# Moving the load of a group's raw weight half from the middle of the following iteration's transfers to the end of an iteration

## The chip, the cores and the metric

The kernel runs on one core of a Trainium2 chip. The metric is device microseconds of one execution. Before the change the median of three runs is 1696.12 us (1695.85 to 1698.0).

## The reference

Two layers of gated cross attention with feed-forward blocks work on `x` (4 batches of 256 tokens, 256 wide) and a context of 1601 tokens per batch. The change lies in the first layer's attention. Cut to what matters:

```python
ln_out = _ln(hidden_states, ln_w, ln_b)
q  = _ln(_fp8_linear_pertensor(ln_out, wq, ...).reshape(b, s, g, hpg, d), qln_w, qln_b)    # 8 groups, 2 heads each, d = 128
k  = _ln(_fp8_linear_pertensor(ln_out, wk, ...).reshape(b, s, g, d), kln_w, kln_b)
v  = _fp8_linear_pertensor(ln_out, wv, ...).reshape(b, s, g, d)
core = _gqa(q, k, v)                                      # softmax(q k^T / sqrt(d)) v over the 256 own tokens
qx = _ln(_fp8_linear_pertensor(ln_out, wqx, ...), qxln_w, qxln_b)
kx, vx = jnp.split(jnp.einsum('bsi,oi->bso', cond, w_kv_x), 2, axis=-1)
xout = _gqa(qx, _ln(kx, kxln_w, kxln_b), vx)              # over the 1601 context tokens
cat = jnp.concatenate([core, xout], axis=-1)
return jnp.einsum('bsi,oi->bso', _div_clamp_fp8(cat, proj_smooth), wproj) * (proj_in_scale * proj_w_scale)
x = x + jnp.tanh(g_xattn[0]) * that
```

The second layer, the mixture of experts and the last feed-forward come after this attention and aren't touched.

## The kernel before

The attention is a software pipeline over `NGB` = 32 pairs of a group of heads and a batch. In the first 16 pairs batches 0 and 1 alternate, so that one group's weights serve two iterations. Each iteration makes the keys, queries and values of the following pair (`it + 1`), and works through the four softmax rounds n = 4·it to 4·it + 3 of its own pair, 128 query rows each against 1601 + 256 keys.

The probabilities of a round lie in `PB[n % 2]` as two bf16 parts. They have to be turned before TensorE can multiply them with the values: `turn_p(n, h)` is a transposing DMA issued from SyncE (L976) that writes half h of round n (h = 0: 16 blocks of 128 x 128, h = 1: 14 blocks) into `PT`. TensorE's `times_v(k, h)` (L1758, 24 matmuls for h = 0 and 21 for h = 1) takes rounds 2k and 2k + 1 together, and waits for `pt{h}_in0` and `pt{h}_in1`, which those DMAs raise. So `times_v(2 it + 1, 0)`, which TensorE meets in iteration it + 1 right after its second group of query projections (L1691), needs `turn_p(4 it + 3, 0)`, which SyncE issues at the start of its iteration it + 1.

Weights come from memory as float32 and have to be split into two bf16 parts once per group. For groups 2 to 7 that is done in halves of 512 columns: `sp_load_half` (L428) loads 512 KB into the single buffer `rawh`; ScalarE (L719, L721, L732, L743), VectorE (L626, L628) and, for the key half, GpSimd (L541, L543) write the two parts into a buffer that the trace calls `acc`; `sp_store_half` (L439 and L440 for the key half, L442 for the query half) stores them to `w_split`. From there `load_weights` (L931) fetches them into `wsb` when their group is due. There are 12 such half loads, one in each of the iterations 0 to 11. A half may be loaded only when the half before it has been split: `sp_load_half` waits on `w_hi`, `w_lo_dve`, `w_hi_pool` and `w_lo_pool`. VectorE's last split of an iteration stands ahead of its last `p_lo` of round 4 it + 2, on which `turn_p(4 it + 2, 1)` waits, and GpSimd's stands ahead of its `split_self` for the same round.

In SyncE's program an iteration is written out by hand. It issues, in this order: `turn_p(4 it - 1, 0)` and `(4 it - 1, 1)`; the V part of the weights if a new group follows; the store of the split half; the load of the next raw half; the K part; `turn_p(4 it, 1)`, `(4 it, 0)`, `(4 it + 1, 0)`; the rows of key norms out and back (L948, L961); the projection weights (L939, every second iteration); `turn_p(4 it + 1, 1)`, `(4 it + 2, 0)`, `(4 it + 2, 1)`; and in the iterations 8 to 19 a context store (L482). All of these go into the one DMA queue of SyncE.

Of the kernel before, what the change touches and what calls it, by code (L numbers as in the profile page):

```python
# [302 lines left out]
def flat(t):  # L303
    return t.rearrange("p a b -> p (a b)")
# [45 lines left out]
def wait_split(e, s, g, keys):  # L350

    e.wait_ge(s["w_hi"], parts_before(g + 1) if not keys else parts_before(g) + 6)
    e.wait_ge(s["w_hi_pool"], plain_before(g + 1))
    e.wait_ge(s["w_lo_dve"], parts_before(g + 1) if not keys else parts_before(g) + 6)
    e.wait_ge(s["w_lo_pool"], plain_before(g + 1))
# [66 lines left out]
def sp_load_half(e, m, s, g, keys):  # L422
    if keys and g > 2:
        wait_split(e, s, g - 1, False)
    elif not keys:
        wait_split(e, s, g, True)
    c0 = CK if keys else CQ
    e.dma_start(m.rawh, m.A["w_all"][g][:, :, c0:c0 + 512]).then_inc(s[f"w_in{int(not keys)}"], 16)  # L428


def sp_store_weights(e, m, s, g):
    wait_split(e, s, g, False)
    e.dma_start(m.w_split[g], (m.wsb if g == 0 else m.wo)[:, :]).then_inc(s["w_out"], 16)


def sp_store_half(e, m, s, g, keys):
    wait_split(e, s, g, keys)
    if keys:
        e.dma_start(m.w_split[g][:, 0:1024], m.woh[:, 0:1024]).then_inc(s["w_out"], 16)  # L439
        e.dma_start(m.w_split[g][:, 3072:4096], m.woh[:, 1024:2048]).then_inc(s["w_out"], 16)  # L440
    else:
        e.dma_start(m.w_split[g][:, 1024:3072], m.woh).then_inc(s["wq_out"], 16)  # L442
# [9 lines left out]
def sp_load_piece(e, m, s, b, i, part):  # L452

    ic, a, z = PIECES[i]
    if part == 0:
        if i == 0 or b == 3:
            e.wait_ge(s["pa_full"], made(first_of(2) - 4 + b, "V3"))
            e.wait_ge(s["ctx_out"], 64 * (b - 1))
        if i:
            wait_split(e, s, G - 1, False)  # L460
            e.wait_ge(s["wq_out"], 16 * (G - 2))
            e.wait_ge(s["ctx_lo_pool"], pieces_before(b, 0))
    k = (0, (z - a + 1) // 2, z - a)
    e.dma_start(ctx_piece(m, b, i)[0][:, k[part]:k[part + 1]], m.A["ctxT"][:, ic, b, a + k[part]:a + k[part + 1]]).then_inc(
        s[f"ctx_in{i}"], 16)
# [19 lines left out]
def sp_store_inputs(e, m, s, j):  # L485
    e.wait_ge(s["xq_done"], j + 1)
    at = QUANT[j % 4] * IC * S
    e.dma_start(m.inputs_d[j // 4][:, at:at + IC * S].rearrange("p (i s) -> p i s", i=IC),
                quantised(m, j)).then_inc(s[f"xq_out{j % 2}"], 16)
# [326 lines left out]
SPLITS = 2 * (G - 2)  # L816
# [19 lines left out]
def group_of(it):  # L836
    return it // 2 if it < PAIRS else it % G
# [7 lines left out]
def new_group(it):  # L845

    return it >= PAIRS or it % 2 == 0


def groups_taken(it):  # L850

    return it // 2 + 1 if it < PAIRS else it - PAIRS // 2 + 1


def made(it, what):

    at = ORDER.index(what)
    if it >= NGB:
        return len(ORDER) * NGB - LAG + it - NGB + 1
    missing = min(it, LAG) + (it < LAG and at >= ORDER.index("PR"))  # L860
    return len(ORDER) * it + at + 1 - missing
# [26 lines left out]
def raw_projection(m, i):  # L888

    return m.wpr[:, :] if i < NGB - 1 else m.rawh.rearrange("p i c -> p (i c)")  # L890
# [28 lines left out]
def sp_attention(e, m, s):  # L919
    w_at = (0, 2 * IC * 256, 2 * IC * 768, 2 * IC * WCOLS)  # L920

    def load_weights(it, which):
        if not 0 < it < NGB or not new_group(it):
            return
        e.wait_ge(s["pa_full"], made(it - 1, ("K3", "Q1", "V3")[which]))
        if it < PAIRS and which == 0:
            e.wait_ge(s["w_out"], 32 * group_of(it) if it > 2 else 32)
        elif 2 < it < PAIRS and which == 1:
            e.wait_ge(s["wq_out"], 16 * (group_of(it) - 1))
        a, b = w_at[which], w_at[which + 1]  # L930
        e.dma_start(m.wsb[:, a:b], m.w_split[group_of(it)][:, a:b]).then_inc(s[("ld_k", "ld_q", "ld_v")[which]], 16)  # L931

    def load_projection(i):
        if not 0 <= i < NGB or not new_group(i):
            return
        if 0 < i < NGB - 1:
            e.wait_ge(s["pw_lo"], groups_taken(i) - 1)
        c = 2 * HPG * group_of(i)
        e.dma_start(raw_projection(m, i), flat(m.A["wprojT"][:, c:c + 2 * HPG, :])).then_inc(  # L939
            s["pw_in" if i < NGB - 1 else "pw_last"], 16)  # L940

    def row_out(it):
        if not it < NGB:
            return
        e.wait_ge(s["kr_pow"], it + 1)
        if it >= 2:
            e.wait_ge(s[f"rs_in{it % 2}"], 16 * (it // 2))
        e.dma_start(m.rs_d[it % 2], m.rr[:, :]).then_inc(s["rs_row"], 16)  # L948

    def row_in(it):  # L950
        if not it < NGB:
            return
        e.wait_ge(s["rs_row"], 16 * (it + 1))
        if it == 0:
            e.wait_ge(s["ln_out"], 2)
        elif it == 1:
            e.wait_ge(s["ctx_lo_dve"], 2 * IC)
            e.wait_ge(s["ctx_lo_pool"], 2 * IC)
        else:
            e.wait_ge(s["mm"], 12 * (it - 1))  # L960
        e.dma_start(m.rsb[it % 2], m.rs_d[it % 2].rearrange("t k -> (t k)")[0:RSC].partition_broadcast(P)).then_inc(  # L961
            s[f"rs_in{it % 2}"], 16)

    def turn_p(n, h):
        if not 0 <= n < 4 * NGB:
            return
        a, b = HALVES[h]
        k = n // 2
        if h == 0:
            e.wait_ge(s["p_lo"], 2 * n + 1)  # L970
        else:
            e.wait_ge(s["p_lo"], 2 * n + 2)
            e.wait_ge(s["s_lo"], n + 1)
        if k >= 2:
            e.wait_ge(s["tv_done"], 2 * (k - 2) + h + 1)
        e.dma_start_transpose(m.PT[k % 2][:, 2 * a // P:2 * b // P, (n % 2) * P:(n % 2 + 1) * P],  # L976
                              m.PB[n % 2][:, 2 * a:2 * b]).then_inc(s[f"pt{h}_in{n % 2}"], 16)

    for it in range(-1, NGB + LAG - 1):
        if it == -1:  # L980
            sp_store_weights(e, m, s, 1)
        if it == 0:
            sp_small(e, m, s)
        if it == NGB - 1:
            sp_reload(e, m, s)
        turn_p(4 * it - 1, 0)
        turn_p(4 * it - 1, 1)
        load_weights(it + 1, 2)
        if 0 < it <= SPLITS:
            sp_store_half(e, m, s, (it + 3) // 2, it % 2 == 1)  # L990
        if 0 <= it < SPLITS:
            sp_load_half(e, m, s, it // 2 + 2, it % 2 == 0)
        for b, i in PIECES_AT.get(it, ()):
            sp_load_piece(e, m, s, b, i, 0)
            sp_load_piece(e, m, s, b, i, 1)
        for j in ROUNDS_OUT.get(it, ()):
            sp_store_inputs(e, m, s, j)
        if it in INPUTS_AT:
            sp_load_inputs(e, m, s, INPUTS_AT[it])
        if 3 * G <= it < 3 * G + 2:  # L1000
            sp_raw_up(e, m, s, it - 3 * G, 0)
        if it == NGB:
            sp_raw_rest(e, m, s)
        load_weights(it + 2, 0)
        if it + 2 >= PAIRS:
            load_weights(it + 2, 1)
        turn_p(4 * it, 1)
        turn_p(4 * it, 0)
        turn_p(4 * it + 1, 0)
        if it + 2 < PAIRS:  # L1010
            load_weights(it + 2, 1)
        row_out(it + 1)
        row_in(it + 1)
        if it < NGB:
            load_projection(it - 1)
        if it == NGB - 1:
            load_projection(NGB - 1)
        turn_p(4 * it + 1, 1)
        if 3 * G <= it < 3 * G + 2:
            sp_raw_up(e, m, s, it - 3 * G, 1)  # L1020
        turn_p(4 * it + 2, 0)
        turn_p(4 * it + 2, 1)
        for b, first in enumerate(STORES_AT):
            if first <= it < first + 4:
                sp_store_context(e, m, s, b, it - first)
# [825 lines left out]
def sp_small(e, m, s):  # L1851
    e.dma_start(m.wg[:, :, :], m.A["wgT"]).then_inc(s["ffn_in"], 16)
    e.dma_start(m.brow[:, :], m.A["ffn_bias"].partition_broadcast(P)).then_inc(s["ffn_in"], 16)
# [10 lines left out]
def sp_reload(e, m, s):  # L1864

    e.wait_ge(s["mm"], 12 * (NGB - 1))
    e.dma_start(m.x[:, :, :], m.A["x"].rearrange("(t p) d -> p t d", p=P)).then_inc(s["x_in"], 16)
# [1039 lines left out]
def sp_program(e, m, s):  # L2907
    sp_prologue(e, m, s)
    sp_attention(e, m, s)
    sp_layer1(e, m, s)  # L2910
# [92 lines left out]
```

## Time and profile before

| what | value |
|---|---|
| median of three runs | 1696.12 us |
| profiled execution, its own time | 1695.35 us |
| its span | 1693.5 us |
| TensorE (PE) busy | 1604.8 us, 95% |
| VectorE (DVE) busy | 1394.1 us, 82% |
| ScalarE (ACT) busy | 1377.3 us, 81% |
| GpSimd (POOL) busy | 1146.5 us, 68% |
| SyncE's DMA queue (q1), share of 16 engines | 70.7% |
| transposing DMAs into `PT` | 256, median 5.2 us from issue to landing |
| loads of `rawh` from `in_w_all` | 12, 512 KB each, median 5.6 us to landing |

The busy shares are averages over the whole program. The change touches only the stretch from about 60 to 490 us, where an iteration of the attention takes some 34.4 us, so the rows below are read iteration by iteration there. SPq is SyncE's queue of DMA issues: a row's duration is how long SyncE was busy issuing, and the landing is when the data had arrived, counted from the start of the issue.

### The profile page before, as it was taken

What the parts mean: (1) busy time and instruction counts of PE and PEld (TensorE: products, weight loads), DVE (VectorE), ACT (ScalarE), POOL (GpSimd) and SP (SyncE); (2) the same over time, 40 slices, a digit from 0 to 9 for tenths busy, and PEclk for the clock granted to TensorE, in tenths of its full rate; (3) what the DMA queues carried; (4) which work ended last, traced back from release to release, by engine and by line L of the source; (5) the groups of instructions that cost most, each with busy time, mean ns of one, the idle gap of its engine ahead of it and who ended that gap; (6) DMA issues with size and microseconds to landing.
All of it is one profiled execution on the core that took longest, in us unless ns stands there. A gap on an engine that the chain in (4) does not pass through costs nothing. (4 is left out here: it accounts for less than half of the span.)

```text
span 1693.5 us, 44076 instructions
## 1 busy us (share of the span) xinstructions
PE 1604.8 (95%) x16026; PEld 1008.1 (60%) x16026; DVE 1394.1 (82%) x3498; ACT 1377.3 (81%) x2311; POOL 1146.5 (68%) x1770
## 2 busy tenths in 40 slices
PE   3799999999999999989999999998898999999998
PEld 1476777777776677767777777766554333333333
DVE  8899999999999989999988888888997765655422
ACT  4688888898888788878888888874346999999997
POOL 3568778787787877778788878875665655646300
PEclk9899999999999999999999999998999999999999
DMA  5299989999989999999999999998523223222100
GB/s 178 81 202 203 195 196 197 199 204 215 199 183 217 214 199 180 222 204 211 200 186 211 227 208 195 206 183 164 175 45 111 45 45 78 45 39 46 33 15 14
DMA packets 608872, 261.11 MB, mean 154 GB/s; under 512 B 576528, under 2 KB 581648, under 8 KB 607248
## 3 DMA queue, kind: packets, MB, share of 16 engines
q1 hardware_dynamic: 604432, 258.05, 70.7%
q8 instruction: 127, 2.08, 0.5%
q10 hardware_dynamic: 4224, 0.25, 0.2%
q14 instruction: 89, 0.73, 0.1%
HBM read 99.15 MB, written 17.29 MB: 69 GB/s over the span
## 5 line engine op out<-in xcount | busy, mean ns | idle before, releaser
L1738 PE MATMUL score<-KK,QT 128*128 128x512 bf16 (+2 forms) x1920 | 342.1, 322 | 7.4 <-DVE mxp L1233 7.4
L1758 PE MATMUL pv<-PT,VV 128*128 128x256 bf16 (+1 forms) x2880 | 338.3, 274 | 6.4 <-DMA PT<-PB 6.4
L1498 ACT ACTIVATE PB<-S,rsum 128x1024 bf16<-128x1024 f32 (+1 forms) x256 | 246.4, 987 | 107.4 <-DVE rsum L1264 82.1
L1758 PEld LDWEIGHTS pv<-PT,VV 128*128 128x128 bf16 (+1 forms) x2880 | 279.8, 98 | 72.1 <-issue 32.1
L1255 DVE SCALAR_TENSOR_TENSOR PB<-S,rsum,PB 128x1024 bf16<-128x1024 f32 (+1 forms) x256 | 295.7, 1156 | 3.2 <-ACT PB L1498 3.2
L1738 PEld LDWEIGHTS score<-KK,QT 128*128 128x128 bf16 x1920 | 157.9, 98 | 146.2 <-DVE mxp L1233 15.1
L1488 ACT ACTIVATE S<-S,nmx 128x1601 f32<-128x1601 f32 x128 | 210.0, 1640 | 7.0 <-DVE nmx L1245 7.0
L2740 ACT ACTIVATE P<-score 128x1024 f32<-128x1024 f32 x196 | 198.0, 1055 | 4.2 <-PE score L2832 3.4
L1076 POOL TENSOR_SCALAR S<-S,rsum 128x256 f32<-128x256 f32 x128 | 70.4, 550 | 126.3 <-DVE rsum L1264 112.4
L1617 PE MATMUL tb<-stage,wsb 128*128 128x512 bf16 (+1 forms) x768 | 148.3, 335 | 7.2 <-DVE stage L635 3.9
L2852 PE MATMUL pv<-P,V 128*9 128x256 f32 (+1 forms) x2288 | 152.2, 380 | 0.3 <-ACT P L2740 0.3
L1098 POOL TENSOR_TENSOR catq<-yt,ym 128x512 bf16<-128x512 f32 x64 | 119.6, 1869 | 0.3
L1233 DVE CUSTOM_DVE_ANT_0 S<-score,rsb 128x1024 f32<-128x1024 f32 (+1 forms) x128 | 104.4, 816 | 11.4 <-PE score L1738 8.5
L1233 DVE CUSTOM_DVE_ANT_0 S<-score,x 128x1024 f32<-128x1024 f32 (+1 forms) x128 | 104.4, 816 | 9.7 <-PE score L1738 7.3
L1617 PEld LDWEIGHTS tb<-stage,wsb 128*128 128x128 bf16 x768 | 66.4, 98 | 72.8 <-issue 7.2
L1442 ACT ACTIVATE kn<-pa,a_nm,a_rs 128x128 f32<-128x128 f32 x256 | 95.6, 455 | 11.7 <-POOL a_nm L1039 11.7
L1088 POOL TENSOR_TENSOR yt<-yq,ym 128x512 f32<-128x512 bf16 x64 | 95.4, 1490 | 13.9 <-DVE ym L1289 9.5
L1658 PE MATMUL tb<-wsb,stage 128*128 128x128 bf16 x1536 | 99.0, 222 | 2.9 <-DVE KK L1166 2.7
L1034 POOL TENSOR_SCALAR a_nm<-a_mv 128x4 f32<-128x4 f32 x64 | 42.0, 656 | 87.5 <-DVE a_mv L1199 87.5
L1080 POOL TENSOR_TENSOR PB<-S,PB 128x256 bf16<-128x256 f32 x128 | 91.5, 715 | 10.9
L1414 ACT ACTIVATE KK<-tb,dcols 128x512 bf16<-128x512 f32 (+1 forms) x128 | 75.9, 593 | 28.0 <-PE tb L1617 28.0
L1658 PEld LDWEIGHTS tb<-wsb,stage 128*128 128x128 bf16 x1536 | 93.4, 100 | 7.1 <-DVE KK L1166 5.2
(286 smaller groups left out, 3685.2 us busy)
## 6 DMA issues: line engine op xcount, KB each, us to landing
x<-rs_d SPq DMA_DIRECT2D x16, 936.0 KB, 5.2
rsb<-rs_d SPq DMA_DIRECT2D x16, 936.0 KB, 5.5
wsb<-w_split SPq DMA_DIRECT2D x46, 256.0 KB, 4.6
wsb<-w_split SPq DMA_DIRECT2D x23, 512.0 KB, 4.9
wpr<-in_wprojT SPq DMA_DIRECT2D x23, 512.0 KB, 6.6
context_d<-stage SPq DMA_DIRECT2D x16, 400.2 KB, 3.8
l_ctx<-context_d SPq DMA_DIRECT2D x4, 1601.0 KB, 7.2
rawh<-in_w_all SPq DMA_DIRECT2D x12, 512.0 KB, 5.6
```

The source lines that it names most:

```text
L1098: e.tensor_tensor(out[:, :, pr * 256:(pr + 1) * 256], m.yt[:, :].rearrange("p (k c) -> p k c", k=2), m.ym[pr][:, :].rearrange("p (k c) -> ...
L1233: e.tensor_tensor_reduce(m.S32[par][:, at:at + b - a], m.score[:, a:b], m.rsb[it % 2][:, key:key + b - a], 1.0, start, ALU.mult, ALU.max, ...
L1255: e.scalar_tensor_tensor(m.PB[n % 2][:, lo:lo + b - a], m.S32[n % 2][:, a:b], m.rsum[n % 2][:, 1:2], m.PB[n % 2][:, 2 * a:a + b], ALU.mult ...
L1442: a = e.activation(m.kn[i][:, k * D:(k + 1) * D], bank[:, k * D:(k + 1) * D], ACT.Identity, bias=m.anm[i][:, k:k + 1], scale=m.ars[i][:, k ...
L1488: e.activation(x, x, ACT.Exp, bias=m.nmx[par][:, 1:2], accum_out=m.sums[par][:, 1:2])
L1498: e.activation(m.PB[n % 2][:, 2 * a:a + b], m.S32[n % 2][:, a:b], ACT.Copy, scale=m.rsum[n % 2][:, 1:2]).then_inc(s["p_hi"], 1)
L1617: r = e.matmul(bank[:, 0:b - a], wk[:, w, ic, D:2 * D], ctx_op(m, it, part, ic, a, b), start=(n == 0), stop=(n == 5))
L1658: r = e.matmul(bank[:, h * D:(h + 1) * D], ctx_op(m, it, part, ic, t * P, (t + 1) * P), wv[:, w, ic, D:2 * D], start=(n == 0), stop=(n == 5))
L1738: i = e.matmul(m.score[:, at:at + b - a], qt[:, kind, qp, q * P:(q + 1) * P], kk[:, kp, a:b], start=(k == 0), stop=(k == 2))
L1758: i = e.matmul(m.pv[:, at:at + 256], vv[0:rows, v, t, :], m.PT[k % 2][0:rows, turned(c, a), :], start=(c == first and r == 0), stop=(c == ...
L2740: e.activation(pr[:, :], bank, ACT.Exp, scale=float(D1) ** -0.5).then_inc(s["l1_exp"], 1)
L2852: r = e.matmul(m.pv[j * R:j * R + VC, 0:S], m.V1[p][0:rows, t, 4 * hq + j, :], probabilities(m, n, j // 2)[0:rows, at:at + S], start=(t == ...
```

## The change

The load of the raw half that belongs to iteration it + 1 is issued at the end of iteration `it`, behind `turn_p(4 it + 2, 1)` and ahead of a context store, where before it stood in iteration it + 1 behind two transposing DMAs, the V load and the store. The very first load, in iteration 0, stays. Eleven loads move; which half is loaded, where to, and what it waits on stay as they were.

```diff
-        if 0 <= it < SPLITS:
-            sp_load_half(e, m, s, it // 2 + 2, it % 2 == 0)
+        if it == 0:
+            sp_load_half(e, m, s, 2, True)
         for b, i in PIECES_AT.get(it, ()):
...
         turn_p(4 * it + 2, 0)
         turn_p(4 * it + 2, 1)
+        if 0 <= it < SPLITS - 1:
+            sp_load_half(e, m, s, (it + 1) // 2 + 2, it % 2 == 1)
         for b, first in enumerate(STORES_AT):
```

SyncE's queue at the border of iterations 0 and 1. The first two rows are `turn_p(2, 0)` and `(2, 1)`, the next transposing pair is round 3, `wsb` is the V load, and `w_split<-acc` are the stores of the split key half:

```order
 L976 DMA_TRANSPOSE PT<-PB 128x16x128 [waits p_lo]
 L976 DMA_TRANSPOSE PT<-PB 128x14x128 [waits s_lo,p_lo]
+L428 DMA rawh<-in_w_all 128x2x512 [waits w_lo_dve,w_lo_pool,w_hi_pool,w_hi]
 L976 DMA_TRANSPOSE PT<-PB 128x16x128 [waits p_lo]
 L976 DMA_TRANSPOSE PT<-PB 128x14x128 [waits s_lo,p_lo]
...
 L439 DMA w_split<-acc 128x1024 [waits w_lo_dve,w_lo_pool,w_hi_pool,w_hi]
 L440 DMA w_split<-acc 128x1024
-L428 DMA rawh<-in_w_all 128x2x512 [waits w_lo_dve,w_lo_pool,w_hi_pool,w_hi]
```

The load has moved ahead of round 3's two transposing DMAs, of the V load and of the two stores.

SyncE's queue at the border of iterations 8 and 9 before, where the first context store stands (iterations 8, 9 and 10 have one at this place beside a moved load):

```order
L976 DMA_TRANSPOSE PT<-PB 128x14x128 [waits tv_done,s_lo,p_lo]
L482 DMA context_d<-stage 128x1601 [waits ctx_lo_pool,ctx_lo_dve]
L976 DMA_TRANSPOSE PT<-PB 128x16x128 [waits tv_done,p_lo]
L976 DMA_TRANSPOSE PT<-PB 128x14x128 [waits tv_done,s_lo,p_lo]
L931 DMA wsb<-w_split 128x1024 [waits pa_full]
L439 DMA w_split<-acc 128x1024 [waits w_lo_dve,w_lo_pool,w_hi_pool,w_hi]
L440 DMA w_split<-acc 128x1024
L428 DMA rawh<-in_w_all 128x2x512 [waits w_lo_dve,w_lo_pool,w_hi_pool,w_hi]
```

And the same place after the change:

```order
L976 DMA_TRANSPOSE PT<-PB 128x14x128 [waits tv_done,s_lo,p_lo]
L428 DMA rawh<-in_w_all 128x2x512 [waits w_lo_dve,w_lo_pool,w_hi_pool,w_hi]
L482 DMA context_d<-stage 128x1601 [waits ctx_lo_pool,ctx_lo_dve]
L976 DMA_TRANSPOSE PT<-PB 128x16x128 [waits tv_done,p_lo]
L976 DMA_TRANSPOSE PT<-PB 128x14x128 [waits tv_done,s_lo,p_lo]
L931 DMA wsb<-w_split 128x1024 [waits pa_full]
L439 DMA w_split<-acc 128x1024 [waits w_lo_dve,w_lo_pool,w_hi_pool,w_hi]
L440 DMA w_split<-acc 128x1024
```

Load and store now both stand between `turn_p(34, 1)` and `turn_p(35, 0)`. No instruction moves on the other engines.

## Rows read from the trace of the kernel before

**Rows 1.** The page: busy time and share of the span of each engine.
```profile
PE 1604.8 (95%) x16026; PEld 1008.1 (60%) x16026; DVE 1394.1 (82%) x3498; ACT 1377.3 (81%) x2311; POOL 1146.5 (68%) x1770
```

**Rows 2.** Windows: one iteration with weight splitting, one late iteration without (columns named).
```profile
core 0: us, PE busy (x) PEld busy (x) DVE busy (x) ACT busy (x) POOL busy (x), PEclk, DMA share, GB/s
266.06:300.50 34.44, 34.25 (x315) 24.98 (x313) 32.52 (x85) 31.63 (x70) 28.89 (x35) 1.00 0.94 192
840.50:874.55 34.05, 34.05 (x314) 25.07 (x313) 30.12 (x80) 28.00 (x51) 26.80 (x30) 1.00 1.02 210
```

**Rows 3.** Waits, 60 to 495 us: total us, times, longest.
```profile
PE score L1738 <- DVE mxp L1233: 3.8, 11, 1.0
```

**Rows 4.** Timeline of SyncE's issues at the border of iterations 5 and 6.
```profile
263.59 14.93 SPq L976 DMA_TRANSPOSE PT<-PB  x5
278.69 0.98 SPq L442 DMA_DIRECT2D w_split<-acc  x1
279.84 0.57 SPq L428 DMA_DIRECT2D rawh<-in_w_all  x1
285.92 7.42 SPq L976 DMA_TRANSPOSE PT<-PB  x3
```

**Rows 5.** L976, one issue each with landing, and TensorE's timeline: borders 0, 5, 6, 8, 9.
```profile
L976 SPq DMA_TRANSPOSE PT<-PB x1: 2840/2840/2840, 101.3 to 101.3; - x1
DMA to landing us min/median/max: 6.8/6.8/6.8
108.96 0.49 PE L1758 MATMUL pv<-PT,VV 128*128 128x256 bf16 x3
...
L976 SPq DMA_TRANSPOSE PT<-PB x1: 2242/2242/2242, 274.4 to 274.4; - x1
DMA to landing us min/median/max: 4.6/4.6/4.6
281.46 0.49 PE L1758 MATMUL pv<-PT,VV 128*128 128x256 bf16 x3
...
L976 SPq DMA_TRANSPOSE PT<-PB x1: 1543/1543/1543, 311.9 to 311.9; - x1
DMA to landing us min/median/max: 5.7/5.7/5.7
319.56 0.50 PE L1758 MATMUL pv<-PT,VV 128*128 128x256 bf16 x3
...
L976 SPq DMA_TRANSPOSE PT<-PB x1: 3085/3085/3085, 377.5 to 377.5; - x1
DMA to landing us min/median/max: 5.8/5.8/5.8
384.77 0.49 PE L1758 MATMUL pv<-PT,VV 128*128 128x256 bf16 x3
...
L976 SPq DMA_TRANSPOSE PT<-PB x1: 3557/3557/3557, 411.7 to 411.7; - x1
DMA to landing us min/median/max: 5.5/5.5/5.5
419.19 0.38 PE L1758 MATMUL pv<-PT,VV 128*128 128x256 bf16 x2
```

**Rows 6.** Timeline of SyncE's issues, the context store of iteration 8.
```profile
376.32 1.11 SPq L482 DMA_DIRECT2D context_d<-stage  x1
```

**Rows 7.** L976: a transposing DMA behind `rsb` alone (230.2), and behind `x` and `wpr` (263.6).
```profile
L976 SPq DMA_TRANSPOSE PT<-PB x1: 2000/2000/2000, 230.2 to 230.2; - x1
DMA to landing us min/median/max: 6.4/6.4/6.4
...
L976 SPq DMA_TRANSPOSE PT<-PB x1: 3063/3063/3063, 263.6 to 263.6; - x1
DMA to landing us min/median/max: 9.1/9.1/9.1
```

**Rows 8.** The page's DMA issues, and L541, the first reader of the load of 279.84.
```profile
rawh<-in_w_all SPq DMA_DIRECT2D x12, 512.0 KB, 5.6
...
L541 POOL CAST acc<-rawh x2: 288/786/1285, 287.7 to 288.5; 128x128 bf16<-128x128 f32 x2
```

## The prediction

> **What bounds the kernel now.** I read the page first: TensorE is busy 95% of the span and no other engine comes near [rows 1]. Then windows of one iteration each. An iteration with weight splitting takes 34.44 us and TensorE works in 34.25 of them, at a granted clock of 1.00; a late iteration without splitting takes 34.05 us with TensorE busy for all of it, 314 matmuls [rows 2]. So TensorE sets the pace, and an iteration of the changed stretch is already within 34.44 - 34.05 = 0.39 us of the one in which TensorE never stops. About half of that 0.39 us is known: TensorE waits for VectorE's row maximum before a score block, 3.8 us in 11 waits between 60 and 495 us [rows 3]. Nothing of that is a wait for weights or for the queue.
>
> The DMA queue is nearly full in the same windows: its share is 0.94 of 16 engines [rows 2]. SyncE's issues come in two bursts with a calm stretch between. At the border of iterations 5 and 6 the timeline shows five transposing DMAs issued almost without a gap from 263.59 to 278.52, then the store at 278.69, the raw load at 279.84, and the next transposing DMA only at 285.92, as it waits for VectorE's next probabilities [rows 4]. The load now fills that calm stretch: with 5.6 us to landing [rows 8] it is in at 285.4. The change takes it out of the calm stretch and puts it into the burst, ahead of the last two transposing DMAs.
>
> **The change part by part.**
>
> *Its own wait.* The load waits until the half before it is split. In its new place it stands behind `turn_p(4 it + 2, 1)`, which waits on work that VectorE and GpSimd do after their last split of the iteration (front matter: their program order). So the wait is met on arrival, and I cost it at nothing. The gaps behind it are those of issue and transfer.
>
> *What it removes.* 11 loads leave the calm stretch. Nobody waited for them there: the first reader of the load of 279.84, landed at 285.4, is GpSimd's L541 at 287.7 [rows 8], and it is neither late nor preceded by a wait for a DMA; the next transposing DMA waits for VectorE, not for SyncE. Removing them is worth 0. Landing 5 us earlier is worth 0 for the same reason: the readers stand where they stand in their engines' orders.
>
> *What it adds.* 11 times `turn_p(4 it + 3, 0)`, and with it `(4 it + 3, 1)`, the V load and the stores, go out behind 512 KB more. What is late next is TensorE's block of `pv` that reads the turned rows. Its margin is the block's start less the landing [rows 5]:
>
> - border 0: 101.3 + 6.8 = 108.1, needed at 108.96: 0.9 us
> - border 5: 274.4 + 4.6 = 279.0, needed at 281.46: 2.5 us
> - border 8: 377.5 + 5.8 = 383.3, needed at 384.77: 1.5 us
> - border 9: 411.7 + 5.5 = 417.2, needed at 419.19: 2.0 us
> - border 6, second half: 311.9 + 5.7 = 317.6, needed at 319.56: 2.0 us
>
> Borders 1, 2, 3, 4, 7 and 10 repeat the pattern of border 5 with margins of its size or more. The V load has a larger margin, as its reader comes behind both `pv` blocks.
>
> *How much later, d.* No row shows a raw load in this place. Bounds: below, 0, where SyncE has a gap to issue it in and the queue runs dry meanwhile. Above, the projection load of the same 512 KB, which every second iteration goes out right ahead of a transposing DMA: that one lands 9.1 us after its issue, and the one with only the row of key norms ahead 6.4 us: 2.7 us [rows 7]. Between them lies the context store, 400 KB, which in the iterations 8 and 9 takes exactly the place that the load will have. It costs SyncE 1.11 us of issue [rows 6]. From the first issue behind `turn_p(4 it + 2, 1)` to the landing of `(4 it + 3, 0)` it takes 7.0 us at border 8, where that issue is the store (376.3 to 383.3); without a store it takes 4.6 us at border 5, but 6.8 us at border 0 [rows 5, 6]. So 400 KB cost from 0.2 to 2.4 us, the middle 1.3; times 512/400 that is 1.7. The load's own issue is shorter (0.57 us [rows 4]), which takes nothing off if the transfer is what counts. I take d = 2.0, between this and the 2.7, as both are of its kind. Ring order decides that it is paid at all: the Trainium skill, "DMA: Bandwidth & Descriptors", section "Queues, rings and completion order", says that each DMA engine consumes the descriptors of one queue in ring order, which speaks against this change, since the load can't be overtaken by the transposing DMAs behind it. The same page's section "Where 436 GB/s comes from" gives about 358 GB/s for transfers from memory; by it 512 KB would be an estimated 1.5 us and the sum below would be 0.6 us.
>
> *The sum.* A TensorE wait is d less the margin where that is positive, and counts in full, since TensorE is the bound and VectorE waits for this very `pv`. With d = 2.0: border 0 1.1, border 8 0.5, borders 9 and 6 0.1 together, others 0. Sum +1.7 us. The profiled execution, 1695.35 us, would become 1697.05; the median of the runs lies 0.8 above the profiled one, so the prediction is 1696.12 + 1.7 = 1697.8 us. With d = 2.7: 1.8 + 0.2 + 1.2 + 0.7 + 0.7 = 4.6 us, and up to 0.2 us at each of the six unshown borders, so some 5 us. With d = 0: no change. At borders 8 to 10 the load and a store are both ahead, which the margins of 8 and 9 already hold for the store.
>
> **The rivals.**
>
> 1. *Hidden altogether.* Before the transposing DMA in question SyncE often waits a little for VectorE, and the load may be issued and drained there: then d is under 0.9 and nothing waits. 1696.1 us. For it: 0.57 us of issue is small. Against it: five issues in a row with hardly a gap [rows 4], and a queue at 0.94.
>
> 2. *It costs every iteration.* If mixing a plain load into transposing DMAs costs more than its bytes, d is over the 2.7 of [rows 7]. At d = 3.3: 2.4 + 0.8 + 1.8 + 1.3 + 1.3 = 7.6, and six others at about 0.6 = 3.6, some 11 us: 1707 us. The point from which the result is slower than noise, +3.4 us, is d of about 2.5. For it: the 2.7 us. Against it: the context store, with three quarters of the bytes, leaves margins of 1.5 and 2.0 us.
>
> 3. *Faster.* The 0.39 us per iteration that TensorE loses to VectorE [rows 2] would have to shrink: VectorE, GpSimd or the transposing DMAs of the calm stretch would have to run quicker once the load is no longer there. If all of it went, 11 x 0.39 = 4.3 us: 1691.8 us. It decides the sign only where it outweighs the waits of the sum, so above 0.15 us an iteration. For it: the queue is empty when `turn_p(4 it, 1)` starts. Against it: the wait in [rows 3] follows work on VectorE (splits, probabilities), and the load has landed before that DMA starts even now (285.4 against 285.92).
>
> **How the numbers follow.** A measurement of this kernel tells about 0.2%, 3.4 us, from no change. The forecast (waits of 0.5 to 3.4 us in sum) gets 0.44, hidden altogether 0.25, costs every iteration or at least more than 3.4 us 0.23, faster 0.08, of which 0.06 by more than 3.4 us or for a reason that I don't see. Slower by over 0.2%: 0.24; within: 0.70; faster: 0.06. The range leaves out the far end of rival 2 and most of rival 3: 1694.6 to 1702.0 us, the upper end being 1696.12 + 5 for d = 2.7 with 0.9 for the scatter of the runs.
>
> **What would show it.** In the profile after: the raw loads stand behind `turn_p(4 it + 2, 1)`, without a wait of their own; `turn_p(4 it + 3, 0)` lands about 2 us later, counted from the first issue behind `turn_p(4 it + 2, 1)`; "pv waits for the DMA into `PT`" appears in TensorE's waits with 1 to 3 us over two to four times, the largest in the iteration that starts near 95 us, the next near 385; other iterations keep 34.4 us. The splits by ScalarE, VectorE and GpSimd start where they did. The prediction is wrong if every iteration between 95 and 455 us gets longer (d too small), if none shows a `pv` wait (d too large), or if the waits for VectorE's row maximum change their size (rival 3).

## The result and the profile after

The changed kernel takes 1701.49 us, the median of 8 runs (1697.92 to 1704.36), against 1695.98 us for the kernel before in the same comparison (8 runs, 1693.87 to 1698.0): a ratio of 1.0034, with a 95% interval from 1.0024 to 1.0044. That is 5.5 us slower, where I had forecast 1.7. The profiled execution took 1702.09 us with a span of 1700.2 us, 6.7 us over the span before.

The page's line on the engines answers to [rows 1]. The number of instructions is the same. TensorE's busy time is 5.7 us larger, but most of that lies ahead of the changed stretch (see the windows below):

```profile
PE 1610.5 (95%) x16026; PEld 1010.0 (59%) x16026; DVE 1394.5 (82%) x3498; ACT 1377.9 (81%) x2311; POOL 1144.4 (67%) x1770
```

TensorE's waits between 95 and 460 us, where the moved loads act, in the kernel before (total us, times, longest):

```profile
PE score L1738 <- DVE mxp L1233: 3.5, 10, 1.0
...
```

The same view and stretch after:

```profile
PE score L1740 <- DVE mxp L1235: 5.3, 10, 1.1
PE pv L1760 <- DMA PT<-PB: 4.9, 4, 1.5
...
```

A new row stands there, the `pv` wait for the DMA into `PT`: 4.9 us in four times. The waits for the row maximum grew by 1.8 us. (The third row of both views, 0.5 us for `kn`, is the same. Line numbers are two higher after the change. Border b is the place between the iterations b and b + 1.) TensorE's timeline has the four waits, at the borders 0, 4, 8 and 9; the bracket is the idle time before the block and what ended it:

```profile
110.78 1.47 PE L1760 MATMUL pv<-PT,VV 128*128 128x256 bf16 x12 [0.77 <-DMA PT<-PB]
250.43 2.78 PE L1760 MATMUL pv<-PT,VV 128*128 128x256 bf16 x24 [1.31 <-DMA PT<-PB]
390.73 2.78 PE L1760 MATMUL pv<-PT,VV 128*128 128x256 bf16 x24 [1.28 <-DMA PT<-PB]
426.84 1.36 PE L1760 MATMUL pv<-PT,VV 128*128 128x256 bf16 x11 [1.52 <-DMA PT<-PB]
```

SyncE's queue at the border of iterations 5 and 6, which answers to [rows 4], and then at that of 8 and 9. The load stands in its new place, after the last `turn_p` of round 4 it + 2, and waits for nothing:

```profile
265.04 11.05 SPq L976 DMA_TRANSPOSE PT<-PB  x3
276.26 0.94 SPq L428 DMA_DIRECT2D rawh<-in_w_all  x1
277.30 5.58 SPq L976 DMA_TRANSPOSE PT<-PB  x2
...
375.95 4.70 SPq L976 DMA_TRANSPOSE PT<-PB  x2
380.81 1.00 SPq L428 DMA_DIRECT2D rawh<-in_w_all  x1
381.90 0.56 SPq L482 DMA_DIRECT2D context_d<-stage  x1
382.55 6.20 SPq L976 DMA_TRANSPOSE PT<-PB  x2
```

The issue and landing of `turn_p(4 it + 3, 0)` behind it answer to [rows 5]: borders 0, 4, 8 and 9.

```profile
L976 SPq DMA_TRANSPOSE PT<-PB x1: 4009/4009/4009, 103.1 to 103.1; - x1
DMA to landing us min/median/max: 7.5/7.5/7.5
...
L976 SPq DMA_TRANSPOSE PT<-PB x1: 3922/3922/3922, 242.7 to 242.7; - x1
DMA to landing us min/median/max: 7.5/7.5/7.5
...
L976 SPq DMA_TRANSPOSE PT<-PB x1: 4531/4531/4531, 382.6 to 382.6; - x1
DMA to landing us min/median/max: 8.0/8.0/8.0
...
L976 SPq DMA_TRANSPOSE PT<-PB x1: 4682/4682/4682, 417.8 to 417.8; - x1
DMA to landing us min/median/max: 8.9/8.9/8.9
```

At border 4 it lands at 242.7 + 7.5 = 250.2 us and `pv` starts at 250.43. Windows of whole iterations beside [rows 2]: the one with that wait takes 35.90 us, the next one 34.40, as before. TensorE is idle for 35.90 - 34.42 = 1.48 us of the first.

```profile
core 0: us, PE busy (x) PEld busy (x) DVE busy (x) ACT busy (x) POOL busy (x), PEclk, DMA share, GB/s
229.20:265.10 35.90, 34.42 (x315) 24.89 (x313) 32.52 (x85) 29.74 (x60) 27.29 (x32) 1.00 0.90 179
265.10:299.50 34.40, 34.20 (x314) 24.96 (x312) 32.50 (x85) 30.34 (x63) 27.26 (x33) 1.00 0.95 200
```

**Where the 6.7 us are.** I cut both profiled executions at the starts of the same `pv` blocks. Windows of the kernel before:

```profile
0.00:91.31 91.31, 49.69 (x369) 31.98 (x369) 75.22 (x191) 54.09 (x118) 45.49 (x82) 0.87 0.44 134
91.31:445.76 354.45, 350.45 (x3170) 254.11 (x3171) 334.67 (x867) 308.26 (x622) 279.64 (x323) 1.00 0.95 201
...
724.90:1163.06 438.16, 429.22 (x3873) 314.39 (x3874) 390.41 (x1004) 353.32 (x624) 339.53 (x372) 0.99 0.98 203
```

And after:

```profile
0.00:92.20 92.20, 53.47 (x368) 33.59 (x369) 75.18 (x190) 54.10 (x117) 45.41 (x82) 0.83 0.43 133
92.20:454.13 361.93, 351.24 (x3169) 253.75 (x3170) 337.34 (x867) 308.42 (x622) 275.23 (x323) 1.00 0.95 197
...
732.96:1168.36 435.40, 429.17 (x3875) 314.73 (x3874) 388.20 (x1002) 352.13 (x622) 341.05 (x372) 0.99 0.99 204
```

The stretch in which the moved loads act takes 7.5 us more, 361.93 against 354.45. TensorE works 0.8 us more there and is idle for 10.7 instead of 4.0 us. The same stretch takes 354.38 us in experiment 1 below. Block by block the difference grows in steps: 0.9 us at border 0, 1.5 at border 4, 0.2 at border 6, 0.8 in iteration 7, 1.45 at border 8, 1.7 at border 9 and 0.7 in iteration 10; 5.7 of them at `pv` blocks behind the DMA, 1.5 at two score blocks that wait for the row maximum. The steps add up to 7.3 and miss the 7.5 by rounding and small drifts. The first stretch is 0.9 us longer, where no moved load acts yet: there the granted clock was 0.83 against 0.87, which also makes TensorE's busy time 3.8 us larger. The late stretch, in which no moved load acts, is 2.8 us shorter; the two stretches that aren't shown differ by -0.3 and +1.4 us. All of these I count as scatter of single executions, which no run here tests; the difference of the medians, 5.5 us, is the better size of the whole.

**The delay itself.** I take it as one number for each border: from the end of the issue of `turn_p(4 it + 2, 1)` to the landing of `turn_p(4 it + 3, 0)`. At border 0 after the change it is 103.1 + 7.5 less the end of the issues before the load, 101.9, which makes 8.7 us. "fetch" says whether the queue of TensorE's instructions (q8 on the page) moved one of its 16 KB blocks within that time.

| border | before | after | d | fetch before / after |
|---|---|---|---|---|
| 0 | 6.8 | 8.7 | 1.9 | yes / yes |
| 1 | 5.1 | 7.0 | 1.95 | no / no |
| 2 | 5.3 | 8.8 | 3.5 | no / yes |
| 3 | 5.0 | 7.4 | 2.4 | no / no |
| 4 | 5.0 | 8.8 | 3.8 | no / yes |
| 5 | 4.65 | 7.3 | 2.65 | no / no |
| 6 | 5.5 | 7.5 | 2.05 | no / no |
| 7 | 5.85 | 7.6 | 1.7 | yes / yes |
| 8 | 7.1 | 9.95 | 2.9 | no / yes |
| 9 | 6.8 | 10.9 | 4.1 | yes / yes |
| 10 | 6.6 | 8.6 | 2.0 | no / no |

The mean d is 2.6 us. Where the fetch is the same before and after, leaving out border 9, it is 2.1 us over seven borders; where a fetch came in, it is 2.9 to 3.8.

### The profile page after: what moved, and what is told of

It reads as the page before. It is cut to its first block and busy times, and to the rows that moved or that the text cites. A ratio compares the mean times of both kernels' runs of the same rounds, so it can differ in the third digit from the quotient of the medians.

```text
span 1700.2 us, 44076 instructions
## 1 busy us (share of the span) xinstructions
PE 1610.5 (95%) x16026; PEld 1010.0 (59%) x16026; DVE 1394.5 (82%) x3498; ACT 1377.9 (81%) x2311; POOL 1144.4 (67%) x1770
## 5 line engine op out<-in xcount | busy, mean ns | idle before, releaser
L1257 DVE SCALAR_TENSOR_TENSOR PB<-S,rsum,PB 128x1024 bf16<-128x1024 f32 (+1 forms) x256 | 299.1, 1169 | 4.1 <-ACT PB L1500 4.0
L1082 POOL TENSOR_TENSOR PB<-S,PB 128x256 bf16<-128x256 f32 x128 | 91.4, 714 | 10.9
```

The source lines that it names most:

```text
L1257: e.scalar_tensor_tensor(m.PB[n % 2][:, lo:lo + b - a], m.S32[n % 2][:, a:b], m.rsum[n % 2][:, 1:2], m.PB[n % 2][:, 2 * a:a + b], ALU.mult ...
```

## The experiments

**1. The load behind round 4 it + 3.** Is it being ahead of that pair that costs, or being out of its old place?

```diff
         turn_p(4 * it - 1, 1)
+        if 0 < it < SPLITS:
+            sp_load_half(e, m, s, it // 2 + 2, it % 2 == 0)
...
         turn_p(4 * it + 2, 1)
-        if 0 <= it < SPLITS - 1:
-            sp_load_half(e, m, s, (it + 1) // 2 + 2, it % 2 == 1)
```

> The eleven loads stand at the start of the following iteration, behind both transposing DMAs of round 4 it + 3 and ahead of the V load and the store. Theory A (queue order: what costs is only what stands ahead of the transposing DMAs of round 4 it + 3): their landings go back to those of before, no pv wait beyond the one near 92 us, 1696 us, ratio 0.999 to 1.001. Rival B (a load issued within the burst costs wherever it stands, since the DMA engines are full): about half or more of the loss stays, 1699 us or more.

Measured: 1696.49 us (11 runs) against 1695.46, ratio 1.0008 [1.0000, 1.0017]. This is what theory A expected. The delays at the eleven borders are those of before within 0.5 us, and no `pv` block waits between 95 and 460 us. The waits of TensorE there:

```profile
PE score L1740 <- DVE mxp L1235: 3.5, 10, 0.9
...
```

Both the `pv` waits and the growth of the row maximum's wait are gone. The load is out of the old place here too, and ahead of the V load and the stores, so the cost is that of standing ahead of the two transposing DMAs.

**2. The load between the two halves of round 4 it + 3.**

```diff
         turn_p(4 * it - 1, 0)
+        if 0 < it < SPLITS:
+            sp_load_half(e, m, s, it // 2 + 2, it % 2 == 0)
         turn_p(4 * it - 1, 1)
```

(The load at the end of the iteration is taken out as in experiment 1.)

> The loads stand between the two transposing DMAs of round 4 it + 3. Theory A: half 0 lands as before; half 1 lands 2 to 4 us later, against margins of 2 to 4 us: waits only ahead of the second pv block, at borders 0, 2, 4 and 6, by 0 to 1 us each, 1696 to 1699 us. Rival B: as in the changed kernel, 1701 us.

Measured: 1700.28 us (5 runs), ratio 1.0032 [1.0020, 1.0044], above what was expected. Half 0 lands as before (within 0.35 us at ten borders), half 1 from 1.2 to 4.4 us later, and the waits have moved to the second `pv` block. TensorE's waits between 60 and 495 us:

```profile
PE score L1740 <- DVE mxp L1235: 6.2, 12, 1.0
...
PE pv L1760 <- DMA PT<-PB: 2.7, 4, 1.1
```

Of the 2.7 us one wait, 0.9 us, stands ahead of the first moved load, as it does in the kernel before. The other three are 0.5, 0.2 and 1.1 us at the borders 6, 8 and 10: about the size that I expected, but of the places 0, 2, 4 and 6 only one was right. What I had not counted is the row maximum: 6.2 us against 3.8 in [rows 3]. So besides the wait of a late `pv` itself, some iterations lose time once more at the score block that waits for VectorE.

**3 and 4. Almost no bytes, in the new place and in the old.** Apart from the very first load, 16 of the 512 columns are loaded, so all but 16 columns of the raw weights are left out; the splits work on what was in the buffer. Experiment 3 makes the edit in the changed kernel, experiment 4 in the kernel before.

```diff
-    e.dma_start(m.rawh, m.A["w_all"][g][:, :, c0:c0 + 512]).then_inc(s[f"w_in{int(not keys)}"], 16)
+    n = 512 if (g, keys) == (2, True) else 16
+    e.dma_start(m.rawh[:, :, 0:n], m.A["w_all"][g][:, :, c0:c0 + n]).then_inc(s[f"w_in{int(not keys)}"], 16)
```

> The changed kernel with the eleven moved loads cut to 16 of 512 columns (16 KB); the other columns of the buffer keep old numbers, so weights of groups 2 to 7 are wrong and only the time counts. Theory A (bytes in the queue): the transposing DMAs land nearly as before, no new pv waits, 1696 to 1697 us. Rival C (the issue slot and the change from transposing to plain transfers cost, not the bytes): half or more of the loss stays, 1699 us or more.

> The kernel before with its loads in the old place cut to 16 of 512 columns, as in the run before it; weights of groups 2 to 7 are wrong, only the time counts. If the load in the calm stretch is free: 1696 us, ratio 0.999 to 1.001. Rival D (it had a price there too, by traffic beside the engines' work): 1693 us or less.

Measured: in the new place 1695.25 us (12 runs), ratio 1.0002 [0.9993, 1.0012]; in the old place 1694.77 us (12 runs), ratio 1.0005 [0.9992, 1.0017]. (The ratios are not quotients of the medians. The intervals are what to read.) SyncE's queue of experiment 3 at border 0 shows that the instruction still takes its slot of 0.96 us:

```profile
92.62 8.03 SPq L977 DMA_TRANSPOSE PT<-PB  x3
100.82 0.96 SPq L429 DMA_DIRECT2D rawh<-in_w_all  x1
101.83 5.27 SPq L977 DMA_TRANSPOSE PT<-PB  x2
```

Of the time the slot costs nothing that can be measured, the bytes cost all of it. Of the delay the slot is a part: it grew by 0.0 to 0.8 us at ten borders, 0.5 in the mean, and by 2.3 at border 4, where a fetch came in. And taking the bytes out of the calm stretch gains nothing: the load was free there, and rival 3 has nothing to win from its removal.

**5 and 6. Only the borders with the late landings, and only the others.** `moved(it)` says at which borders the load is moved; at the rest it stands in its old place. Experiment 6 has `not in` for `in`.

```diff
+def moved(it):
+    return it in (0, 4, 8, 9)
...
-        if it == 0:
-            sp_load_half(e, m, s, 2, True)
+        if it == 0 or 0 < it < SPLITS and not moved(it - 1):
+            sp_load_half(e, m, s, it // 2 + 2, it % 2 == 0)
...
-        if 0 <= it < SPLITS - 1:
+        if 0 <= it < SPLITS - 1 and moved(it):
```

> Only the loads at borders 0, 4, 8 and 9 are moved, those at which the changed kernel's trace has pv waits of 0.8 to 1.5 us; the other seven stay in the old place. Theory A (each border pays its own wait, landing delay less margin): nearly the whole loss, 1700 to 1702 us, ratio 1.0025 to 1.004. Rival E (the loss is a small cost at every border, for instance of the busier burst on the other engines): 4/11 of it, about 1698 us.

> The complement: the loads at borders 1, 2, 3, 5, 6, 7 and 10 are moved, those at 0, 4, 8 and 9 stay in the old place. Theory A: 1696 to 1697.5 us, a wait of some tenths at border 6 and perhaps one of VectorE's longer instructions behind it. Rival E: 7/11 of the loss, about 1699.5 us.

Measured: the four borders alone 1698.56 us (12 runs) against 1695.63, ratio 1.0022 [1.0012, 1.0033]; the other seven 1695.43 us (12 runs), ratio 0.9996 [0.9987, 1.0004]. For the four borders I had expected 1700 to 1702; taken alone, 1698.56 is what rival E forecasts, and it is experiment 6 that refutes that rival, which expects 1699.5 there. TensorE's waits between 95 and 460 us and its timeline in experiment 5:

```profile
PE pv L1764 <- DMA PT<-PB: 2.3, 3, 1.2
...
109.87 2.78 PE L1764 MATMUL pv<-PT,VV 128*128 128x256 bf16 x24 [1.21 <-DMA PT<-PB]
248.99 2.78 PE L1764 MATMUL pv<-PT,VV 128*128 128x256 bf16 x24 [0.89 <-DMA PT<-PB]
```

The seven other loads are free although they delay their landings by 1.5 to 3.7 us: their margins hold it, up to one wait of 0.2 us at border 2. The four carry 2.9 of the 5.5 us. The trace of experiment 5 shows what is missing: at border 8 the wait is 0.2 us instead of 1.3, and at border 9 there is none. The delays there grew by 2.2 and 2.3 us only, not by 2.9 and 4.1; at border 8 the block of instructions that fell into the transfer in the changed kernel comes at 390.9 us, after the landing at 387.05. The three `pv` waits, 2.3 us, and 0.7 us more of waits for the row maximum (4.2 against 3.5) make up the 2.9. So the two parts don't add up to the whole in these profiles, because with the other seven loads in their old place the later fetches fall elsewhere. Each profile is one execution, and the intervals of the two parts (2.0 to 5.6 us and -2.2 to 0.7) don't exclude the 5.5 us, so this is read and not tested.

**7. The load two issues earlier, ahead of round 4 it + 2.** If a delay is paid only by the pair right behind the load, this place should be free.

```diff
+        if 0 <= it < SPLITS - 1:
+            sp_load_half(e, m, s, (it + 1) // 2 + 2, it % 2 == 1)
         turn_p(4 * it + 2, 0)
         turn_p(4 * it + 2, 1)
-        if 0 <= it < SPLITS - 1:
-            sp_load_half(e, m, s, (it + 1) // 2 + 2, it % 2 == 1)
```

> The eleven loads stand two places earlier than in the changed kernel, ahead of both transposing DMAs of round 4 it + 2. Theory A with a queue that drains in the gap of about 1 us before round 4 it + 3: the landing of its half 0 is delayed by less than in the changed kernel, by 1 to 2 us instead of 2 to 4; smaller waits, 1697 to 1699 us. Theory A with a queue that never drains: the same landing as in the changed kernel, 1701 us. Nothing else waits for round 4 it + 2 so soon.

Measured: 1696.11 us (12 runs), ratio 1.0001 [0.9991, 1.0010], faster than both theories expected. Counted from the end of the issue before, the delay of `turn_p(4 it + 3, 0)` is back within 0.5 us of before at eight borders (0.9 and 1.3 us less at 0 and 7, 1.9 more at 4). But that issue itself ends 0.8 to 3.0 us later against TensorE, as the load now stands ahead of it. Counted against TensorE's `pv` block, the landing is still 0.5 to 1.9 us later than in the kernel before at nine borders, and 3.5 and 3.3 us later at the borders 4 and 9 (mean 1.5 us; in the changed kernel 2.4). So only about a third of the delay is made up before the next pair. The rest fits into the margins, at the borders 0 and 4 with 0.1 us to spare. One `pv` block waits in the profiled execution, at border 9:

```profile
420.97 2.78 PE L1760 MATMUL pv<-PT,VV 128*128 128x256 bf16 x24 [1.52 <-DMA PT<-PB]
```

The place is free as far as the times can tell, but not because the pair behind it lands as before.

**8. Half the bytes in the new place.** 256 of the 512 columns are loaded, the other half of the raw weights is left out.

> The changed kernel with the eleven moved loads cut to 256 of 512 columns (256 KB); the other columns keep old numbers, only the time counts. Theory A with a delay in proportion to the bytes: 1.0 to 1.9 us later at each border, waits of 0.3 at border 0 and 0 to 0.5 at borders 4, 8, 9: 1696.5 to 1698 us. If the delay is mostly a fixed price of a plain transfer amid transposing ones: 1700 us or more.

Measured: 1694.82 us (12 runs), ratio 0.9999 [0.9989, 1.0008], below what was expected; the delay grew by 0.6 to 2.6 us, 1.2 in the mean, and no `pv` block waited. The cost is not in proportion to the bytes: half of them cost nothing, all of them 5.5 us. It is what exceeds the margin; at the borders 0 and 8 it was just enough, with 0.1 us left.

**9 and 10. Shifting the fetches of TensorE's instructions.** In the table above the fetches fall on the even borders up to 4, where d is large when one comes in. Here 48 small extra matmuls, whose result nobody reads, stand before the first scores; they shift every later 16 KB block of TensorE's program by a part of an iteration. Experiment 9 does it in the changed kernel, experiment 10 in the kernel before.

```diff
         queries(it + 1, 0)
+        if it == -1:
+            for _ in range(48):
+                e.matmul(m.pv[:, 0:8], m.ident[:, :], m.ident[:, 0:8], start=True, stop=True)
```

> The changed kernel with 48 small unused matmuls added while TensorE is idle near 20 us; they shift by some 190 instructions where in an iteration TensorE's instruction blocks are fetched (the single 16 KB transfers on the instruction queue), some 10 us earlier. Theory F (the delay is larger at even borders, 8.7 to 8.8 us against 7.0 to 7.4 from the end of the issue before to landing, because such a fetch falls between issue and landing there and stops the transposing transfers for some 1.4 us): the alternation turns round or moves, long landings wherever a fetch falls in. Rival G (it belongs to which half is loaded, or to the projection weights in every second iteration): even borders stay the long ones.

> The same 48 matmuls in the kernel before. No wait at the borders in either theory, within the scatter of single runs 1694 to 1698 us. Theory F: border 0 (6.8 us from the end of the issue before to landing, where the others without a context store take 4.6 to 5.9) falls to about 5 us, as its fetch moves away.

Measured, one execution each: 1714.86 us and 1707.43 us, against 1694.11 for the kernel before. Experiment 10 was expected at 1694 to 1698 us and without waits; both were missed. The added matmuls are not hidden: at border 0 TensorE is already some 10 us later. And two `pv` blocks wait, 1.3 us in all. So only the delays are read. Issue and landing of `turn_p(4 it + 3, 0)` in experiment 9, at border 0 (now without a fetch) and border 1 (now with one):

```profile
L976 SPq DMA_TRANSPOSE PT<-PB x1: 3922/3922/3922, 112.6 to 112.6; - x1
DMA to landing us min/median/max: 6.1/6.1/6.1
...
L976 SPq DMA_TRANSPOSE PT<-PB x1: 3830/3830/3830, 146.3 to 146.3; - x1
DMA to landing us min/median/max: 7.4/7.4/7.4
```

The whole pattern turned round. Delays at the borders 0 to 7 in us:

| kernel | 0 | 1 | 2 | 3 | 4 | 5 | 6 | 7 |
|---|---|---|---|---|---|---|---|---|
| changed | 8.7 | 7.0 | 8.8 | 7.4 | 8.8 | 7.3 | 7.5 | 7.6 |
| experiment 9 | 7.3 | 8.85 | 7.2 | 8.7 | 7.1 | 8.7 | 7.2 | 8.6 |
| experiment 10 | 5.1 | 5.4 | 5.2 | 6.7 | 5.1 | 6.6 | 5.1 | 6.5 |

With a fetch the delay is 8.6 to 8.9 in experiment 9, without one 7.1 to 7.3: a fetch adds 1.5 us. Experiments 9 and 10 have the same fetches at every border except 1, where the block comes so late in experiment 10 that it hardly meets the transfer. Over the other ten borders their difference is the load's own d: 1.9 to 2.2 us at nine, 2.7 at border 9.

The waits did not go away with the fetches. TensorE waits 4.3 us for `PT` in experiment 9 too, 2.0 of them at border 8, where no fetch falls into the delay of 9.0 us. There SyncE's burst stood 1.4 us later against TensorE than in the kernel before (1.3 in experiment 10), and a block had come at 383.6 us (383.2), further ahead in the same burst.

## Why the prediction was right or wrong

**The mechanism: right.** Most of the loss is TensorE's wait for the turned probabilities of round 4 it + 3, paid only beyond the margin. Experiments 1, 3, 6 and 8 each take away one part of it (the place, the bytes, the tight borders, half the bytes) and each gives the time of before within its interval. The rest, 1.5 of the 7.3 us in the profile, are waits for the row maximum, which the sum didn't have. The time fell within the range, near its upper end, and the outcome, 0.34% slower, is in the case that I had given 0.24, not in the likeliest. (The rival behind that case stands with 0.23 in the same paragraph.) That it is within the range is partly luck: the sum said 1.7 us.

**Its own wait, and what it removes: right.** The load waits for nothing in the new place, and experiment 4 shows that its old place was free. The splits keep their place: GpSimd's first reader stands at 291.2 us in the row below, against 287.7 in [rows 8]; TensorE is 3.4 us later there as well.

```profile
L541 POOL CAST acc<-rawh x2: 288/788/1288, 291.2 to 291.9; 128x128 bf16<-128x128 f32 x2
```

**The term that failed is d.** I took 2.0 us, the same at each border, between the 1.7 scaled from the context store and the 2.7 of [rows 7]. Measured it is 2.6 in the mean and 1.7 to 4.1. The load's own part was sized well: 2.1 where the fetches are alike, 1.9 to 2.2 at nine borders in experiments 9 and 10. What was missing is a second term, the fetch of TensorE's instructions, 1.5 us, which hits the borders by chance of position: three of eleven before, six of eleven after. In the kernel before, the blocks at 175.7 and 244.6 us come 1.1 and 1.2 us after the landings of the borders 2 and 4; a landing that is 2 us later meets them. The tell was in my own numbers: border 0 took 6.8 us where border 5 took 4.6, and I put that into the spread of the context store's cost instead of asking for its cause. The sum with the upper bound, d = 2.7, gave some 5 us, close to the 5.5 that came out, but for a partly different reason.

**The margin was taken as fixed.** I had predicted 1.1 us at border 0, 0.5 at border 8, 0.1 at border 9 together with border 6, and nothing at border 4. The waits come out to 0.1 us with a second term that the sum didn't have: how much later the burst as a whole stands against TensorE (the end of the issue before the load, less the start that the `pv` block would have without its wait, each against the kernel before). The fifth column is d less margin plus this term.

| border | d | margin before | burst later by | excess | wait |
|---|---|---|---|---|---|
| 0 | 1.9 | 0.9 | -0.35 | 0.6 | 0.77 |
| 4 | 3.8 | 3.6 | 1.0 | 1.2 | 1.31 |
| 8 | 2.9 | 1.5 | -0.25 | 1.15 | 1.28 |
| 9 | 4.1 | 1.9 | -0.8 | 1.4 | 1.52 |

The store beside the load was paid for in the margins, as predicted: without a fetch of TensorE d is 1.9 at border 8 in experiments 9 and 10 and 2.0 at border 10. What came on top was the fetch.

**The borders that I did not show: wrong at one.** I wrote that borders 1, 2, 3, 4, 7 and 10 repeat border 5 and left them out. Their margins in the kernel before are 2.6 to 3.7 us, as I said. Yet border 4 cost 1.31 us, the second-largest. Its margin is 247.04 - 243.4 = 3.6 us, from the landing and from this row of the kernel before:

```profile
247.04 1.15 PE L1758 MATMUL pv<-PT,VV 128*128 128x256 bf16 x9
```

Two things ate it: d was 3.8 with the fetch, and the whole burst began 1.0 us late against TensorE, as in the table; ahead of it the key norms' way out took 4.5 us instead of 3.5. The first is supported by experiment 9, where border 4 loses its fetch, falls to 7.1 us and has no wait, though its burst is 1.2 us late; that the norms are the reason for the second is read from this one execution.

**A wait counts in full: right, and other waits came beside it.** The iteration with the 1.31 us wait is 1.50 us longer than the next. (The prediction says that the row maximum explains about half of the 0.39 us of an iteration. The wait in that iteration is 0.19 us, which fits; the mean over the 11 of [rows 3] is 0.35.) But the score blocks at 345.58 and 452.82 us wait 1.00 and 0.97 us for the row maximum, which cost 1.5 us on top. I had named a change of these waits as a sign that I was wrong, thinking of a gain; they grew. VectorE's timeline before and after, ahead of the first of them:

```profile
327.52 1.78 DVE L628 SCALAR_TENSOR_TENSOR acc<-rawh,win,acc 128x256 bf16<-128x256 f32 x2
329.22 1.22 DVE L1255 SCALAR_TENSOR_TENSOR PB<-S,rsum,PB 128x640 bf16<-128x640 f32 x1
```

```profile
331.17 2.03 DVE L628 SCALAR_TENSOR_TENSOR acc<-rawh,win,acc 128x256 bf16<-128x256 f32 x2
333.13 1.78 DVE L1257 SCALAR_TENSOR_TENSOR PB<-S,rsum,PB 128x640 bf16<-128x640 f32 x1
```

The same two rows take 0.8 us more. GpSimd runs beside them in both kernels, here before and after:

```profile
327.65 1.37 POOL L1088 TENSOR_TENSOR yt<-yq,ym 128x512 f32<-128x512 bf16 x1
...
329.85 1.62 POOL L1050 TENSOR_TENSOR QT<-t,QT 128x512 bf16<-128x512 f32 x1
```

```profile
331.03 1.15 POOL L1090 TENSOR_TENSOR yt<-yq,ym 128x512 f32<-128x512 bf16 x1
...
333.01 1.22 POOL L1052 TENSOR_TENSOR QT<-t,QT 128x512 bf16<-128x512 f32 x1
```

Before the change VectorE's row starts 0.13 us ahead of GpSimd's and GpSimd is the slow one (1.37 and 1.62 us); after it GpSimd's starts 0.14 us ahead, takes 1.15 and 1.22 us, and VectorE is the slow one. Between 95 and 470 us the L1257 instruction on 128x640 takes 1.78 us or more five times after the change; its like in the kernel before, L1255, never does. In experiments 2, 5, 6 and 7 one of 1.78 to 1.85 us stands 12 to 13 us ahead of a new wait of 0.8 to 1.0 us; experiment 1 has neither. That the order of the start decides who is slowed is my reading of these traces, not a tested cause, and not every slow one is followed by a long wait. Experiment 6 has one such wait, 0.98 us, in its profile without a median above that of before, so what these waits cost stays open.

**The rivals.** Hidden altogether fell: it needed d under 0.9, and no border has less than 1.7. Faster fell with experiment 4. Costs every iteration came true in part: its threshold, d of about 2.5 for a loss over 3.4 us, was passed in the mean. Yet its picture, each iteration longer, did not come: seven of the eleven borders show no `pv` wait, and experiment 6 moves seven loads at no cost. Of a d of 2.6 the load's place in the queue is 2.1 and the fetches are the rest; nothing in the runs asks for a further price of mixing plain and transposing transfers.

**The ring order** that I cited from the Trainium skill ("DMA: Bandwidth & Descriptors", "Queues, rings and completion order") agrees with the runs: what stands behind the load lands later, what stands ahead of it does not (experiment 1 for the pair, experiment 2 for half 0). By the 358 GB/s of the same page of the Trainium skill ("Where 436 GB/s comes from") d would be an estimated 1.5 us; measured it is 2.1, so the measurement decides. Of the 2.1 the load of 16 columns already costs part: against experiment 3, over the eight borders with the same fetches, the remaining bytes add 1.6 us.

## What to carry to other kernels

Price a transfer that moves ahead of others at each place where it lands, not at one typical place: compare the margin of every reader with the delay, since what is lost is the excess alone, and four places out of eleven had all the `pv` waits here. The margin moves too: at border 4 by 1.0 us to the bad. Where the same DMA takes 4.6 us at one border and 6.8 at another, find the reason before averaging over it. A big load is free in a calm stretch of the queue or behind the urgent transfers, and where it has to go ahead of some, ahead of those with the latest readers.

## What the runs showed of the hardware

**A fetch of instructions stops transposing DMAs.** The DMA view of the changed kernel at border 0, in slices of 0.08 us (tenths busy, then GB/s), and the row of the instruction queue: packets, MB, share of 16 engines.

```profile
DMA  9999999999990000000000000004999999999999
GB/s 291 291 288 291 291 288 480 272 256 74 22 19 0 0 0 0 0 3 6 6 10 10 10 10 10 10 10 90 285 279 261 288 291 291 288 291 282 282 294 294
...
q8 instruction: 1, 0.02, 1.9%
```

For about 1.2 us, from 108.5 to 109.7, the 16 engines are idle but for a trickle of 10 GB/s, while a transposing DMA stands half done. The one 16 KB block of instructions starts at 107.99 and takes 0.96 us, so the stop begins 0.5 us behind its start and outlasts it by 0.7. It is no single case: in the kernel before, between 98 and 490 us, the engines move under 40 GB/s for 1.0 us or more with a transfer of SyncE outstanding 14 times, and each of these stops begins 0.3 to 1.1 us behind the start of such a block. At border 2 the same picture comes again; in the kernel before, which has no fetch there, the transfer runs through. It costs the transfer that it hits 1.5 us, as experiments 9 and 10 measured. That the queue is TensorE's shows in them too: 48 matmuls more for TensorE alone moved its blocks. The Trainium skill, "Runtime: NRT & Kernel Launch", section "Instruction fetch mechanics", says that each engine's program is refilled in blocks of 16 KiB by a DMA queue of its own and that the cost of crossing a block is mostly hidden. The trace agrees for TensorE itself: its blocks are there, and none of its waits between 95 and 460 us is for one. But the data transfers in the same DMA engines pay, which only the measurement shows.

**The cost follows position.** 48 matmuls at the start of a program decide which iterations' transfers get hit 100 to 400 us later. Experiment 10, the kernel before with these matmuls, has two `pv` waits of 1.3 us together between 95 and 460 us, where the kernel before has none. So two versions of a kernel that differ in a few instructions can differ by waits of 1 to 2 us, and a profile of one of them doesn't tell where the waits of the other are.
